# Where the output projection's pieces stand in the last batch of a two-layer transformer kernel

## The reference

```python
x = x + a_alpha * attention(ada_rmsnorm(x))      # 16 heads of width 16
x = x + f_alpha * (silu(h @ gate_w.T) * (h @ hidden_w.T) @ out_w.T + out_b)
# h = gamma * rmsnorm(x) + beta, hidden width 1024
```

## Time and profile before

| | |
|---|---|
| three executions | 994.68, 994.97, 996.43 us |
| the profiled execution | 994.97 us |
| its span in the trace | 993.1 us |
| TensorE, matmuls | 965.3 us busy, 5411 instructions |
| VectorE | 727.9 us |
| ScalarE | 552.2 us |
| POOL | 271.6 us |
| mean granted clock of TensorE | 0.998 |

### The profile page before, as it was taken

The page is one execution under the profiler, slowest core; times in us unless marked ns, Lnnn a source line. Parts: engine busy times, 40 slices in busy tenths (PEclk is TensorE's granted clock), DMA queues, the critical chain, the costliest instruction groups (busy, mean ns, idle before and its releaser), DMA issues.

```text
span 993.1 us, 15671 instructions
## 1 busy us (share of the span) xinstructions
PE 965.3 (97%) x5411; PEld 603.8 (61%) x5411; DVE 727.9 (73%) x1216; ACT 552.2 (56%) x1160; POOL 271.6 (27%) x260
## 2 busy tenths in 40 slices
PE   5999999999999999999999999999999999999998
PEld 4777777776534555655664565556556655655577
DVE  5888888999577777678777767876776777677343
ACT  5466554554655656466556646554764665466632
POOL 1265422221101132222213222231222133134142
PEclk9999999999999999999999999999999999999999
DMA  9645556343431122133021302301230213020000
GB/s 285 150 121 126 139 129 160 96 120 78 107 91 30 65 80 45 41 100 70 1 87 55 70 13 96 90 15 67 73 71 4 84 44 60 30 90 7 2 27 22
DMA packets 93742, 75.45 MB, mean 76 GB/s; under 512 B 44880, under 2 KB 79768, under 8 KB 93664
## 3 DMA queue, kind: packets, MB, share of 16 engines
q1 hardware_dynamic: 81344, 61.36, 22.8%
q10 hardware_dynamic: 12320, 13.09, 5.4%
HBM read 27.73 MB, written 12.61 MB: 41 GB/s over the span
## 4 chain that ended last, share of the span: by engine, by line
PE 86%; DVE 7%; issue 2%; ACT 2%; DMA 2%; ACTq 1%; SPq 0%; POOL 0%; DVEq 0%; POOLq 0%
PE bank L1247 20%; PE bank L370 13%; PE bank L1002 12%; PE bank L1021 12%; PE bank L1291 9%; PE raw_pair L926 5%; PE bank L851 4%; PE bank L902 2%; PE bank L1084 2%; DVE amax L452 2%; PE bank L393 2%; DVE h L422 1%; PE bank L401 1%; PE bank L1397 1%; DVE rowmax L958 1%
## 5 line engine op out<-in xcount | busy, mean ns | idle before, releaser
L1010 ACT ACTIVATE probs<-bank 128x512 f32<-128x512 f32 x512 | 277.0, 598 | 172.1 <-PE bank L1002 165.9
L958 DVE TENSOR_REDUCE rowmax<-raw_pair 128x2 f32<-128x1024 f32 x224 | 273.7, 1222 | 114.8 <-PE raw_pair L926 114.8
L370 PE MATMUL bank<-up_w,xs_part 128*128 128x512 f32 x768 | 191.9, 403 | 5.4 <-issue 3.6
L1002 PE MATMUL bank<-q_stack,k_stack 50*128 50x512 f32 x512 | 189.4, 449 | 2.3 <-ACT probs L1010 1.7
L370 PEld LDWEIGHTS bank<-up_w,xs_part 128*128 128x128 f32 x768 | 142.2, 190 | 39.9 <-issue 6.6
L926 PE MATMUL raw_pair<-k_stack,q_stack 48*128 48x512 f32 x448 | 157.7, 449 | 0.4 <-DVE rowmax L958 0.3
L1277 POOL TENSOR_TENSOR hid<-scratch,hid 128x512 fp32r<-128x512 f32 x64 | 82.4, 1288 | 195.4 <-ACT hid L1273 195.4
L1021 PE MATMUL bank<-probs,v_ext 128*17 128x512 f32 x1024 | 134.8, 598 | 0.9 <-issue 0.9
L1002 PEld LDWEIGHTS bank<-q_stack,k_stack 50*128 50x128 f32 x512 | 76.9, 185 | 84.0 <-issue 51.1
L1291 PEld LDWEIGHTS bank<-out_w,hid 128*128 128x128 f32 x672 | 81.4, 188 | 30.0 <-issue 30.0
L1291 PE MATMUL bank<-out_w,hid 128*128 128x256 f32 x672 | 92.0, 287 | 0.0
(11 more groups left out here) (185 smaller groups left out, 1332.3 us busy)
## 6 DMA issues: line engine op xcount, KB each, us to landing
q_stack<-split SPq DMA_DIRECT2D x54, 128.0 KB, 3.0
q_stack<-hid SPq DMA_DIRECT2D x42, 128.0 KB, 2.9
k_stack<-hid SPq DMA_DIRECT2D x42, 128.0 KB, 2.9
xk<-xT SPq DMA_DIRECT2D x32, 128.0 KB, 2.8
xt<-x_tok SPq DMA_DIRECT2D x32, 128.0 KB, 2.6
x_spill<-x1t ACTq DMA_DIRECT2D x32, 128.0 KB, 2.5
xa_spill<-xa ACTq DMA_DIRECT2D x32, 128.0 KB, 2.3
x_in<-xa_spill SPq DMA_DIRECT2D x8, 512.0 KB, 5.2
```

The costliest lines, as they stand in the source:

```text
L370: last = nc.tensor.matmul(bank[j][:], xs_part[a][:, m % 2, k, :], up_w[w][:, k, col + j * W:col + (j + 1) * W], start=(i == 0), stop=(i == ...
L958: nc.vector.reduce_max(rowmax[:, e:e + RAWS + 1:RAWS], raw_pair[:], AX.X).then_inc(raw_read, 1)
L1002: nc.tensor.matmul(score_bank[c % 3][:], k_stack[rows, slot, kt * P:(kt + 1) * P], q_stack[rows, slot, :], start=True, stop=True).then_inc ...
L1010: nc.scalar.activation(probs[:, (kt % 2) * J + j, :], score_bank[c % 3][:], ACT.Exp).then_inc(exp_done, 1)
```

## The change

The last batch's loop takes its output pieces from OUT_PIECES too, but only the first five: (0,0), (2,0), (0,1), (1,0), (1,1) at h = 24 to 28, and none at h = 29, 30 and 31. Before, they were (0,0), (0,1), (1,0), (1,1) at h = 25, 27, 29 and 31. Behind the loop there remain three pieces in place of four: (2,1) in the place of (2,0), and (3,0), (3,1) in the place of (2,1), (3,0), (3,1). The fill ahead of the transposes has six matmuls in place of two. On VectorE the scaling of batch 6's second output half moves from behind the normalised rows to ahead of the mean.

```diff
-        LAST_PIECES = ((0, 0), (0, 1), (1, 0), (1, 1), (2, 0), (2, 1), (3, 0), (3, 1))
-        LAST_OUT_AT = (25, 27, 29, 31)
+        LAST_PIECES = 5
@@ plan
-                if following:
-                    for n, pieces in enumerate(OUT_PIECES):
-                        table[OUT_AT + n] = [("out", t, half) for t, half in pieces]
-                else:
-                    for h, (t, half) in zip(LAST_OUT_AT, LAST_PIECES):
-                        table[h] = [("out", t, half)]
+                for n, pieces in enumerate(OUT_PIECES if following else OUT_PIECES[:LAST_PIECES]):
+                    table[OUT_AT + n] = [("out", t, half) for t, half in pieces]
@@ pe_after
-            rest = LAST_PIECES[len(LAST_OUT_AT):]
+            rest = [piece for pieces in OUT_PIECES[LAST_PIECES:] for piece in pieces]
             for t, half in rest[:1]:
                 out_pe(pe, B - 2, t, half, LAST_OUT)
...
             for t, half in rest[1:]:
                 out_pe(pe, B - 2, t, half, LAST_OUT)
-            fill_last(pe, 2)
+            fill_last(pe, 6)
             xf_pe(pe, B - 1, (END, END), last_normed_rows)
@@ dve_after
             affine_dve(dve, B - 1)
+            out_dve(dve, B - 2, 1, LAST_OUT)
             mean_dve(dve, B - 1)
             normed_dve(dve, B - 1, x1_in, last_normed_rows)
-            out_dve(dve, B - 2, 1, LAST_OUT)
             last_xf_dve(dve)
```

## The result

The changed kernel is slower. In runs side by side it took 1000.34 us (median of five, 999.6 to 1004.39) against 996.03 for the kernel before (five, 994.68 to 996.43): ratio 1.0055, 95% interval 1.0033 to 1.0078. All later comparisons have the kernel before beside them too (medians 995.55 to 996.07), so that its 994.97 us, on which the forecast was built, was one of its better executions. The profiled execution of the changed kernel took 1002.91 us, with a span of 1001.0.

What follows compares the result with a forecast made beforehand. TensorE's order was taken to bound the last loop half-steps, then a chain over VectorE, ScalarE and POOL. 4.74 - 1.88 + 0 + 1.31 + 0 = +4.17 us on 994.97 gave 999.1 us, range 997.2 to 1001.0.

Steps and rivals of the forecast that it cites:

- step 5: VectorE's scaling ahead of the mean waits for the pieces and delays the mean: +1.31 us; POOL's addition no later.
- rival A: New TensorE idle time in half-steps 29 to 31 and ahead of the transposes drops the clock: 1000.6 us; chance 0.18.
- Step 1: Last batch's loop: three more pieces on TensorE before h = 29, 1.58 us each, +4.74 us.
- Step 2: Half-steps 29 to 31 without pieces: last values start 4.53 us after h = 29 starts, before 6.41; gives back 1.88.
- The recurrence: Start-by-start count of scores, exponentials and values in half-steps 29 to 31, giving 4.53 us to the last values.
- Steps 3 and 4: One piece swapped while the heads' output is turned; two pieces, not three, behind the last projection: zero gain or cost.
- Step 6: Six filling matmuls instead of two ahead of the transposes: hidden, zero; up to 0.92 us if the covering wait were gone.
- one of the prediction's own signs of being wrong: Behind 941 us, the granted clock leaving 1.00 would show the forecast wrong.
- Rival B: At VectorE's mean: the scaling does not hold it, only the loop's +2.86 us counts, 997.8 us; chance 0.07.
- C: Even half-steps of the loop have 1.58 us of slack that hides a piece: not slower, 995.0 us; chance 0.05.
- D: ScalarE keeps up better or worse in half-steps 29 to 31: 996.9 or 1000.1 us; chance 0.07 outside the others.

Runs made afterwards that it cites:

- the spread one: Changed kernel with its five last-batch loop pieces at h = 25, 27, 28, 29, 31 instead of packed at 24 to 28: 999.32 us, ratio 1.0033.

## Why the prediction came out as it did

The direction was right, and so was the mechanism of the terms that the sum has. Two terms that it put at nothing failed: in step 5, POOL's addition beside VectorE's normalised rows (+0.69 us), and the clock, which was left to rival A (+1.77 us in the profiled execution). The size was 4.17 us on the trace; the stretches show 6.26 in the profiled execution and 4.62 where the clock did not fall. The median of 1000.34 lies in the range, the profiled execution, 1002.91, outside.

That execution is 7.94 us above 994.97, 3.77 more than forecast: 1.77 for the clock, 1.64 for the later start of the first stretch (cause open), 0.69 for POOL's addition and 0.04 outside the span, less 0.13 in the loop and 0.24 at the mean, which were charged too much. The medians differ by 4.31 us. That this is so near 4.17 is partly luck: in the profile without falls the loop and the mean came out 0.25 us lower than forecast together, which hides a part of POOL's 0.7, and the interval of the ratio lets the difference be anything from 3.3 to 7.8 us.

- Step 1, three pieces on the engine that sets the pace: 4.74 forecast, 4.73 measured. The places and the piece count were tested apart, and both act.
- Step 2, half-steps 29 to 31: 4.53 forecast, 4.41 measured. The recurrence put every wait in its place (fourth score, values, last values); it was 0.10 us late at the values of h = 30 (1.77 us behind the start of h = 29, measured 1.67) and kept that to the end. Loop together: +2.86 forecast, +2.73.
- Steps 3 and 4, the piece in the gap and the shorter cover: zero, as forecast (4.12 us with the clock at 1.00).
- Step 5, the mean behind the scaling: +1.31 forecast, +1.16 (5.12 - 3.96) in the execution without falls. The scaling itself holds the mean for 0.61 us where I charged 0.73.
- Step 5 failed in one sentence: "So it and the last fetch and store behind it are no later", the only thing I asked about POOL's addition. I worked out that it would start at 953.76 on the old clock of events, and VectorE's normalised rows at the same moment, and did not ask whether the two disturb each other. They do: +0.69 us. Parting them removed it, and adding the order alone to the kernel before made it (2.95 us from mean to transposes, as in the changed kernel). The Trainium skill, SBUF — State Buffer, section "SBUF: two separate sides", has the rule: VectorE and GpSimd share a port pair as "an **exclusive lock**, not a bandwidth split", held for a whole instruction by whichever started first; for VectorE this goes for instructions in a two-port mode or with two inputs in SBUF. Our trace agrees for this pair of instructions, of which POOL's started first: 1350 ns in place of 341, ending 0.15 us behind POOL's end. No run shows which mode the VectorE instruction was in.

  The kernel before already had a long VectorE instruction beside POOL:

```profile
931.10 1.18 DVE L1045 TENSOR_TENSOR o_pair<-o_tok,inv_sum 128x256 f32<-128x256 f32 x1
945.34 0.42 DVE L1045 TENSOR_TENSOR o_pair<-o_tok,inv_sum 128x256 f32<-128x256 f32 x1
```

  The first ran while POOL's last product did (930.71 to 932.00), the second with POOL idle; operation and shape are the same. VectorE had nothing else to do until 942.33, so it cost nothing there, but it could have warned of the meeting behind the loop. No run parts this pair.
- Step 6, six fills hidden: right, and 0.92 us where the cover is missing, as priced.
- Rival A, the clock, was given 0.18 and 1.5 us for a fall. In the profiled execution it fell twice: +1.35 us ahead of the other heads' projection and +0.42 in the last stretch, and so one of the prediction's own signs of being wrong came true. The sum has nothing for it. The argument against it was in part that no new gap is as long as 2.31 us; the wait ahead of the transposes was just that long, and 1.61 with POOL parted, so the term missed in step 5 also lengthened it. Its weight looks too low: of the three profiles with VectorE's new order and the unfilled wait ahead of the transposes in which POOL and VectorE meet, two (the changed kernel, and the order alone) lost 0.4 us in the last stretch, the spread one nothing. How often the first fall comes stays open: the same unfilled holes were followed by a fall in one profile and by none in two others.
- Rival B (mean not held: it came 5.03 us behind the start of the other heads' projection, in place of 3.96) and C (pieces hidden by slack: 4.73 us more before h = 29) are refuted by the stretches, and D (ScalarE faster or slower in 29 to 31) by the 4.41 us.

The forecast was also set on 994.97 us; the kernel before has its median about 1 us higher (996.03 beside the changed kernel), which shifts any absolute number: of the 1.24 us between 999.1 and 1000.34, 1.06 are this.

## What to carry to other kernels

Where two engines alternate, work that fills one engine should be spread so that neither waits: the same five pieces cost 2.1 us more when packed ahead of the half-steps than among them. An instruction that waits for covering work must not stand ahead of the chain it covers. And whoever moves an instruction should look for what it makes run at the same moment on the other engines, not only for what waits for it.

## What the runs showed of the hardware that was not expected

A VectorE tensor_scalar of 128x256 in 32 bits, SBUF to SBUF, took 1350 ns in place of 341 while a POOL tensor_tensor of 128x512 was running, and 0.62 us for two once POOL waited. TensorE's clock fell to 0.50 behind 4.41 us of which TensorE was busy for 2.70, with no single gap over 1.3 us, in the changed kernel; in the executions with the old VectorE order and with the parted POOL the same stretch was followed by 1.00.
